# A decoder layer on one core: VectorE's order in the expert tiles, GpSimd's last copy of rows, and 258 columns read in place of 272

## The chip, the cores and the metric

The kernel runs on one core of one Trainium2 chip. The metric is the device time of one execution in microseconds (us), as the median of several runs. Engines are named as in the profile: PE is TensorE (PEld its weight loads), DVE is VectorE, ACT is ScalarE, POOL is GpSimd, SP is SyncE; a name with a q behind it is that engine's sequencer, which issues DMAs.

## The reference

The input is 128 batches of 128 tokens with 256 features. Each batch goes through causal self-attention (16 heads of 64), a layer norm, masked cross-attention (16 heads of 16) and another layer norm. The last part is a mixture of experts over all 16384 tokens, twice (two groups of 32 experts, each token to 2 experts of each group):

```python
logits = x2 @ router_w
expert_weights, expert_indices = lax.top_k(softmax(logits), 2)
xs = x2[tok]                                   # rows sorted by expert
ys = ragged_dot(silu(gate) * up, wd, group_sizes) * flat_w[order][:, None]
out_g = zeros_like(x2).at[tok].add(ys)
...
x = layernorm(x + (out0 * 2 + out1 * 2) / 4)
```

gate and up are `ragged_dot(xs, wg)` and `ragged_dot(xs, wu)` with 256 x 128 weights, wd is 128 x 256; all is float32.

## The kernel before

The program has two blocks, one after the other.

**The first block** takes the batches in a software pipeline of 137 iterations, each of four sub-steps s = 0 to 3. Attention of batch b is worked on in iteration b and later ones; with lag 4 its tokens' places in the experts' lists are made, and with lag 5 its rows are sent. GpSimd's part of that is three functions. `token_rows(b)` copies the batch's normalised rows into `xrow[b % 2]` four times (one for each of a token's four choices) and adds a code; it first waits until the scatters of batch b - 2, which read the same buffer, have landed (`placed`). `open_blocks(b)` makes the block numbers (`rows_of`) from which VectorE's `place_tokens(b)` makes the rows' places. `scatter(b, s)` issues four indirect DMAs, two at s = 2 and two at s = 3, that write the rows (272 columns: 256 features, code, owner and padding) to the arrays `xs_d` in HBM, sorted into tiles of 128 rows of one expert. After the last batch SyncE loads half of the first group's expert weights (`first_half(sp, 1)`), and the block ends when every engine is done; the second block starts on all engines behind that.

**The second block** takes 576 tiles (288 for each group) in steps n = 0, 1, 2 ..., one tile a step, again as a pipeline. In step n:

- SyncE loads tile n's rows into one of 10 buffers `xg` once the code of tile n - 10 is read (`to_made`). Being only issue work, it runs ahead of the others. It also stores finished sums, and loads later expert weights (`LATER`: eight experts in five pieces, one every third step from steps 60, 110 and 160, and four experts each at steps 299 and 303).
- TensorE transposes tile n (L1200), multiplies tile n - 1 by gate and up (L1208), works out in registers where tile n's weights lie (`find_weights`; in every fourth step it also loads a word from memory), transposes h of tile n - 2 (L1219) and multiplies tile n - 3 by the down weights (L1224).
- ScalarE copies tile n's transpose (L1236), then h's transpose of tile n - 2 (L1240), then makes `gate` of tile n - 1 (L1244), then may issue two DMAs for a combine.
- GpSimd issues the indirect DMA that writes tile n - 3's result `y` to its tokens' rows of `y_d` (L1155), with the places in `to`.
- VectorE copies y of tile n - 3 out of PSUM (L1290) into one of four buffers, and makes the places `to` (L1298) and h of tile n - 1 (L1300).

When all tiles that a batch can have rows in are written, the batch is combined: in every second step n (from step 46 to 300, and from 334 on) VectorE has a sum before y (L1285, first sum, of rows that ScalarE's DMA of four steps earlier brought) and one after y (L1293, second sum). In the second group it also has the layer norm's statistics: `bn_stats` (L1305) and the final scaling (L1319) in the steps without sums, `bn_aggr` and the variance (L1311, L1313) in those with sums, and GpSimd has a power (L1151). All this comes in the order in which the code lists it; each engine takes its instructions in that order.

A y buffer is free when its write of four tiles earlier has landed (`y_out`); the two PSUM banks of y are reused every second step; h's PSUM input is freed by h.

Of the kernel before, what the change touches and what calls it, by code (L numbers as in the profile page):

```python
# [25 lines left out]
ALU = mybir.AluOpType  # L26
# [3 lines left out]
P = 128  # L30
D = 256
# [12 lines left out]
HID = 128  # L44
# [50 lines left out]
def wait(eng, sem, value):  # L95

    if isinstance(value, int) and value <= 0:
        return
    eng.wait_ge(sem, value)
# [55 lines left out]
def decoder_layer(nc, xT, x, cT, mask, wq, wk, wv, wo, xwq, xbq, xwk, xbk, xwv, xbv, xwo, xbo,  # L155
                  r0, g0, u0, d0, r1, g1, u1, d1, out):
    NB = x.shape[0]
    N = NB * P
    TILES = NB * TOPK + E
    NT = NGRP * TILES  # L160
    PACK = 4
    SPARE = 4
    ROW = D + 16
    CODE, OWNER = D, D + 1
    x2_d = nc.dram_tensor("x2_d", (N, D), F32).ap()
    xs_d = [nc.dram_tensor(f"xs{g}_d", (TILES * P, ROW), F32).ap() for g in range(NGRP)]
# [5 lines left out]
    with keep:  # L172
# [48 lines left out]
        with ExitStack() as one:  # L221
            def sb(name, shape, dt=F32):
                return tile(one, name, shape, dt)
# [177 lines left out]
            with nc.Block() as block:  # L401
# [71 lines left out]
                def _(pool):  # L473
# [44 lines left out]
                    def iteration(t):  # L518
                        for s in range(NG):
                            lag, g = taken(s)  # L520
                            if s == 2 and (t.live(1) or t.live(3)):
                                pool.wait_ge(var_ready, t.item(1) + 1)
                                nc.gpsimd.tensor_tensor(rs[:, :], spread_v[:, :], minus_half[:, :], ALU.pow).then_inc(rsqrt_ready, 1)
                            if t.live(lag):
                                c = slice(2 * g, 2 * g + 2)
                                pool.wait_ge(y_high, t.item(lag) * NG + (g + 1))
                                nc.gpsimd.tensor_tensor(yT_p[1][:, c, :], yT[:, c, :], yT_p[0][:, c, :].bitcast(F32), ALU.subtract).then_inc(y_split, 1)  # L527
                            if s == 0 and t.p % 2 and t.live(-3):
                                p = t.pair_slot(-3)
                                pool.wait_ge(x_high, t.pair(-3) + 1)  # L530
                                nc.gpsimd.tensor_tensor(xT_p[p][1][:, :, :, :], xT_s[:, :, :, :], xT_p[p][0][:, :, :, :].bitcast(F32), ALU.subtract).then_inc(x_split, 1)  # L531
                                if t.among(-3, 1):
                                    for n in (2, 3):
                                        weight_low(nc.gpsimd.tensor_tensor, pool, n)
                            if s == 1 and t.live(1):
                                keys, n = xkD[:, t.two(1), :, :, :], t.item(1)
                                pool.wait_ge(moved["xk"], n + 1)
                                for m in range(KC):
                                    last = nc.gpsimd.tensor_tensor(keys[:, m, 1:XHALF, :], spread(keys[:, m, 0, :], 1, XHALF - 1),
                                                                   spread(own_head[:, 1:XHALF], 2, P), ALU.mult)  # L540
                                last.then_inc(xk_others, 1)
                                pool.wait_ge(xk_others, n + 1)
                                nc.gpsimd.tensor_tensor(keys[:, :, 0, :], keys[:, :, 0, :], spread(own_head[:, 0:1], 2, P).broadcast_to([P, KC, P]),
                                                        ALU.mult).then_inc(xk_ready, 1)
                            if s == 2 and t.live(1):
                                pool.wait_ge(x1_ready, t.item(1) + 1)
                                nc.gpsimd.tensor_tensor(x1b[t.two(1)][:, :], x1[t.two(1)][:, :], xbo_s[:, :], ALU.add).then_inc(x1b_ready, 1)
                            if s == 1 and t.live(4):
                                token_rows(t.item(4))
                            if s == 2 and t.live(4):  # L550
                                open_blocks(t.item(4))
                            if t.live(5):
                                scatter(t.item(5), s)

                    def open_blocks(b):

# [24 lines left out]
                    def scatter(b, s):  # L581

                        p = b % 2
                        if s == 2:
                            pool.wait_ge(xrow_ready, b + 1)
                            pool.wait_ge(place_ready, b + 1)
                            pool.wait_ge(cleared, CLEAR * clears_for(b))
                        for j in SCATTERS[s]:
                            nc.gpsimd.indirect_dma_start(  # L589
                                xs_d[j // TOPK][:, :], bass.IndirectOffsetOnAxis(ap=place[p][:, j:j + 1].bitcast(U32), axis=0),  # L590
                                xrow[p][:, j, :], None).then_inc(placed[p], 16)
# [444 lines left out]
        with ExitStack() as two:  # L1036
# [19 lines left out]
            packs = [flat[:, i * (NT // PACK):(i + 1) * (NT // PACK)] for i in (0, 1)]  # L1056
            tabs = sb("tabs", [1, NT // PACK], I32)
            spare_no = sb("spare_no", [P, SPARE])
            xg_s = [sb(f"xg{q}", [P, ROW]) for q in range(NX)]
            to = sb("to", [P, NTO], I32)  # L1060
            xgT = [sb(f"xgT{q}", [P, KC, P]) for q in (0, 1)]
            gate_s = [sb(f"gate{q}", [P, HID]) for q in (0, 1)]
# [32 lines left out]
            def combined(n, group=None):  # L1095

                for g in range(NGRP):
                    b, odd = divmod(n - g * TILES - FIRST, 2)
                    if not odd and 0 <= b < NB and group in (None, g):
                        return g, b, g * NB + b  # L1100
                return None

            with nc.Block() as block:
                @block.sync
                def _(sp):
                    for g in range(NGRP):
                        sp.dma_start(owners[:, g * TILES:(g + 1) * TILES, :],
                                     xs_d[g].rearrange("(n p) d -> p n d", p=P)[0:1, :, CODE:OWNER + 1]).then_inc(owners_in, 16)

                    def iteration(t, n):  # L1110
                        for first, count, piece, after in LATER.get(n, ()):
                            if piece == 0:
                                if n == LAST_CHUNK:
                                    sp.wait_ge(y_made, TILES)
                                sp.wait_ge(moe_in, after * CHUNK_LOAD)
                            load_piece(sp, 1, first, count, piece)
                        if t.live(0):
                            q, g = n % NX, n // TILES
                            wait(sp, to_made, n - NX + 1)
                            sp.dma_start(xg_s[q][:, :], xs_d[g][(n - g * TILES) * P:(n - g * TILES + 1) * P, :]).then_inc(xg_in[q], 16)  # L1120
                        done = combined(n - STORE)
                        if done:
                            g, b, k = done
                            p = k % NS
                            if g:
                                sp.wait_ge(out_ready, b + 1)
                                sp.dma_start(out[b, :, :], sums[p][:, :]).then_inc(stored[p], 16)
                            else:
                                sp.wait_ge(sum_ready, k + 1)
                                sp.dma_start(acc_d[b * P:(b + 1) * P, :], sums[p][:, :]).then_inc(stored[p], 16)  # L1130

                    tiles(iteration)
                    for q in range(NQ):
                        sp.wait_ge(y_out[q], 16 * (NT // NQ))
                    for p in range(NS):
                        sp.wait_ge(stored[p], 16 * (NGRP * NB // NS))
# [122 lines left out]
                def _(dve):  # L1259
# [16 lines left out]
                        return weight[:, b, g * TOPK + j:g * TOPK + j + 1]  # L1276

                    def iteration(t, n):
                        now = combined(n - COMBINE)
                        if now:  # L1280
                            g, b, k = now
# [9 lines left out]
                        if now:  # L1291
                            dve.wait_ge(part_ready, k + 1)
                            v.scalar_tensor_tensor(s[:, :], rows[:, k % NR, 1, :], weight_of(g, b, 1), s[:, :], ALU.mult, ALU.add).then_inc(sum_ready, 1)  # L1293
                        if t.live(1):
                            q, m = t.slot(1), t.item(1)
                            dve.wait_ge(gate_in, m + 1)
                            wait(dve, ht_made, t.item(2))
                            v.tensor_tensor(to[:, m % NTO:m % NTO + 1], xg_s[m % NX][:, CODE:CODE + 1], spare_no[:, m % SPARE:m % SPARE + 1],  # L1298
                                            ALU.max).then_inc(to_made, 1)
                            v.tensor_tensor(h_s[q % 2][:, :], gate_s[q % 2][:, :], GB[q % 2][:, HID:2 * HID], ALU.mult).then_inc(h_in, 1)  # L1300
                        full = combined(n - COMBINE - 1, 1)
                        if full:
                            g, b, k = full
# [66 lines left out]
```

## Time and profile before

| | |
|---|---|
| Median of 3 runs | 4887.19 us (4886.07 to 4888.65) |
| The profiled execution's own time | 4894.84 us |
| Its span, first to last instruction | 4893.1 us |
| First block | 0 to about 3750 us |
| Second block | about 3750 to 4893 us |
| Busy over the span: PE, PEld, DVE, ACT, POOL | 97%, 81%, 77%, 70%, 55% |

The busy shares are means over two blocks with different work. Times of rows are microseconds from the start of the span. A row of the timeline has the start, the duration, engine, line, operation and operands (out <- in), and in brackets how long the engine had been idle and what ended that, as inferred from semaphores. Matmuls are pipelined, and their ends are modelled: a group of matmuls overlaps the next, so distances between starts tell more than durations.

### The profile page before, as it was taken

To read this page: it belongs to the slowest core of one execution; us is meant where nothing else is said; L and a number is where in the kernel's file an instruction comes from. 1 tells how busy PE (TensorE), PEld (TensorE's weight loads), DVE (VectorE), ACT (ScalarE), POOL (GpSimd) and SP (SyncE) were. 2 spreads that over 40 slices of the span, in tenths; PEclk is the share of its full clock that TensorE was granted. 3 is DMA by queue.
4 is the path that set the end of the run, shared out by engine and by line. 5 is a ranking of instruction groups with operands and counts; after the bars stand their busy time and mean duration, and the time that the engine had idled before them with its cause. 6 is when DMAs were issued, how large, how long until landed. Compare 5 with 4: busy or idle time off the path is not lost. (4 is left out here: it accounts for less than half of the span.)

```text
span 4893.1 us, 133371 instructions
## 1 busy us (share of the span) xinstructions
PE 4755.2 (97%) x38848; PEld 3976.5 (81%) x38848; DVE 3782.2 (77%) x18828; ACT 3412.7 (70%) x13380; POOL 2712.7 (55%) x3750
## 2 busy tenths in 40 slices
PE   7999999999999999999999999999995999999998
PEld 6888888888888888888888888888874766676665
DVE  4888888888888888888888888888883455547777
ACT  5788888878878888887887888788783444444443
POOL 3455555555555555555555555555554555556666
PEclk9999999999999999999999999999997999999999
DMA  4121111112112111211211211121125799878888
GB/s 137 62 69 61 58 65 64 57 60 69 58 58 67 62 58 64 65 58 57 67 62 57 67 64 58 61 67 58 58 78 162 255 299 298 273 246 270 273 273 255
DMA packets 477157, 556.18 MB, mean 114 GB/s; under 512 B 55602, under 2 KB 407860, under 8 KB 475956
## 3 DMA queue, kind: packets, MB, share of 16 engines
q1 hardware_dynamic: 350516, 300.08, 19.9%
q0 software_dynamic: 52224, 146.87, 8.0%
q10 hardware_dynamic: 73728, 100.70, 6.8%
q8 instruction: 352, 5.77, 0.5%
q14 instruction: 337, 2.76, 0.2%
HBM read 270.08 MB, written 277.35 MB: 112 GB/s over the span
## 5 line engine op out<-in xcount | busy, mean ns | idle before, releaser
L527 POOL TENSOR_TENSOR yTl<-yT,yTh 128x256 fp32r<-128x256 f32 x512 | 381.7, 745 | 910.7 <-DVE yTh L979 907.6
L756 ACT ACTIVATE prob<-prob,negmax 128x128 f32<-128x128 f32 x2048 | 799.0, 395 | 102.5 <-DVE negmax L827 98.3
L1155 POOL DMA_INDIRECT y_d<-y,to x576 | 593.2, 1030 | 464.6 <-DVE y L1290 447.8
L756 ACT ACTIVATE xprob<-xprob,xnegmax 128x128 f32<-128x128 f32 x2048 | 792.9, 392 | 1.6 <-DVE xnegmax L827 1.6
L1208 PE MATMUL bank<-moe,xgT 128*128 x2304 | 594.6, 381 | 0.0
L589 POOL DMA_INDIRECT xs_d<-xrow,place x512 | 515.9, 1008 | 128.1 <-issue 128.1
L1290 DVE COPY y<-bank 128x256 f32<-128x256 f32 x576 | 244.5, 424 | 407.4 <-PE bank L1224 290.0
L827 DVE CUSTOM_DVE_ANT_0 prob<-bank,causal 128x128 f32<-128x128 f32 x2048 | 471.7, 286 | 34.0 <-PE bank L695 20.9
L774 ACT COPY probT<-bank 128x512 f32<-128x512 f32 x512 | 300.0, 586 | 248.0 <-PE bank L705 181.1
L827 DVE CUSTOM_DVE_ANT_0 xprob<-bank,xmask 128x128 f32<-128x128 f32 x2048 | 470.5, 286 | 1.2 <-remote 1.2
L837 DVE TENSOR_TENSOR prob<-prob,inv 128x512 f32<-128x512 f32 x512 | 438.9, 857 | 20.2
L616 PE MATMUL bank<-xT0h,wqkv 128*128 128x256 f32 x2048 | 401.6, 289 | 26.8 <-POOL xT0l L531 26.0
L1240 ACT COPY hT<-bank 128x128 f32<-128x128 f32 x576 | 153.2, 266 | 391.0 <-issue 208.8
L1208 PEld LDWEIGHTS bank<-moe,xgT 128*128 128x128 f32 x2304 | 394.0, 191 | 30.2 <-issue 0.3
L1236 ACT COPY xgT<-bank 128x256 f32<-128x256 f32 x576 | 214.3, 372 | 292.6 <-PE bank L1200 146.4
L616 PE MATMUL bank<-xT1h,wqkv 128*128 128x256 f32 x2048 | 400.7, 288 | 0.0
L1224 PE MATMUL bank<-moe,hT 128*128 x1152 | 392.9, 423 | 0.5
L807 ACT COPY yT<-bank 128x256 f32<-128x256 f32 x512 | 190.4, 372 | 290.2 <-PE bank L731 189.2
L756 ACT ACTIVATION_READ_ACCUMULATOR prob<-prob,negmax 128x1 f32 x2048 | 391.2, 191 | 0.0
L756 ACT ACTIVATION_READ_ACCUMULATOR xprob<-xprob,xnegmax 128x1 f32 x2048 | 391.0, 191 | 0.0
L844 DVE TENSOR_TENSOR xprob<-xprob,xinv 128x512 f32<-128x512 f32 x512 | 373.2, 729 | 17.6
L686 PE MATMUL bank<-kT,qT 64*128 64x128 f32 x4096 | 366.3, 297 | 0.4 <-DVE xnegmax L827 0.4
(180 smaller groups left out, 14188.3 us busy)
## 6 DMA issues: line engine op xcount, KB each, us to landing
xg<-xs_d SPq DMA_DIRECT2D x576, 136.0 KB
xs_d<-blank SPq DMA_DIRECT2D x248, 272.0 KB
rows<-y_d ACTq DMA_DIRECT2D x256, 256.0 KB
xT_s<-xT SPq DMA_DIRECT2D x128, 128.0 KB
x<-x SPq DMA_DIRECT2D x128, 128.0 KB, 2.0
cT<-cT SPq DMA_DIRECT2D x128, 128.0 KB
x_d<-x SPq DMA_DIRECT2D x128, 128.0 KB, 2.0
sums<-x_d ACTq DMA_DIRECT2D x128, 128.0 KB
```

Source lines behind the costliest of these rows:

```text
L527: nc.gpsimd.tensor_tensor(yT_p[1][:, c, :], yT[:, c, :], yT_p[0][:, c, :].bitcast(F32), ALU.subtract).then_inc(y_split, 1)
L589: nc.gpsimd.indirect_dma_start(xs_d[j // TOPK][:, :], bass.IndirectOffsetOnAxis(ap=place[p][:, j:j + 1].bitcast(U32), axis=0), xrow[p][:, ...
L616: last = nc.tensor.matmul(out_ap, lhs(a, k), rhs(b, k), start=(i == 0), stop=(i == len(todo) - 1))
L686: last = nc.tensor.matmul(SELF_SCORES[h], qT[HALVES[h % 2], t.slot(0), c, :], kT[HALVES[h % 2], key_slot(t.slot(0)), c, :], start=True, st ...
L756: last = nc.scalar.activation(dst[:, h, :], dst[:, h, :], ACT.Exp, bias=src_bias[:, h:h + 1], scale=-1.0, accum_out=acc[:, h:h + 1])
L774: nc.scalar.copy(probT[:, :, :].rearrange("p h q -> p (h q)"), T[:, :]).then_inc(probT_in, 1)
L827: last = nc.vector.tensor_tensor_reduce(dst[:, h, :], heads[h], bias[:, :], -1.0, float("inf"), ALU.add, ALU.min, least[:, h:h + 1])
L837: nc.vector.tensor_tensor(prob[s % 2][:, :, :], prob[s % 2][:, :, :], spread(inv[:, :], 2, P), ALU.mult).then_inc(normed, 1)
L844: nc.vector.tensor_tensor(xprob[s % 2][:, :, :], xprob[s % 2][:, :, :], spread(xinv[:, :], 2, P), ALU.mult).then_inc(xnormed, 1)
L1155: nc.gpsimd.indirect_dma_start(y_d[:, :], bass.IndirectOffsetOnAxis(ap=to[:, m % NTO:m % NTO + 1].bitcast(U32), axis=0), y_s[q][:, :], Non ...
L1208: last = nc.tensor.matmul(GB[q % 2][:, 0:2 * HID], xgT[q % 2][:, k, :], moe_cols[:, bass.ds(gate_up + k * 2 * HID, 2 * HID)], start=(k == ...
L1224: nc.tensor.matmul(YB[q % 2][:, 0:D], hT_s[q % 2][:, :], moe_cols[:, bass.ds(down, D)], start=True, stop=True).then_inc(y_made, 1)
```

## The change

Three edits. In the second block, VectorE makes `to` and h of tile n - 1 as the first work of step n; before, both came behind the first sum, y and the second sum. In the first block, `token_rows` of the last batch moves from s = 1 (ahead of `open_blocks` of the same batch and of the scatters of the batch before) to s = 3 of the same iteration, behind both. And the load of a tile's rows reads 258 of the 272 columns; the `xg` buffers are 258 wide. The rows in HBM keep 272 columns.

```diff
-                            if s == 1 and t.live(4):
+                            if s == 1 and t.live(4) and t.item(4) < NB - 1:
                                 token_rows(t.item(4))
                             if s == 2 and t.live(4):
                                 open_blocks(t.item(4))
                             if t.live(5):
                                 scatter(t.item(5), s)
+                            if s == 3 and t.item(4) == NB - 1:
+                                token_rows(t.item(4))
...
-            xg_s = [sb(f"xg{q}", [P, ROW]) for q in range(NX)]
+            xg_s = [sb(f"xg{q}", [P, D + 2]) for q in range(NX)]
...
-                            sp.dma_start(xg_s[q][:, :], xs_d[g][(n - g * TILES) * P:(n - g * TILES + 1) * P, :]).then_inc(xg_in[q], 16)
+                            sp.dma_start(xg_s[q][:, :], xs_d[g][(n - g * TILES) * P:(n - g * TILES + 1) * P, 0:D + 2]).then_inc(xg_in[q], 16)
...
                     def iteration(t, n):
+                        if t.live(1):
+                            q, m = t.slot(1), t.item(1)
+                            dve.wait_ge(gate_in, m + 1)
+                            wait(dve, ht_made, t.item(2))
+                            v.tensor_tensor(to[:, m % NTO:m % NTO + 1], xg_s[m % NX][:, CODE:CODE + 1], spare_no[:, m % SPARE:m % SPARE + 1],
+                                            ALU.max).then_inc(to_made, 1)
+                            v.tensor_tensor(h_s[q % 2][:, :], gate_s[q % 2][:, :], GB[q % 2][:, HID:2 * HID], ALU.mult).then_inc(h_in, 1)
                         now = combined(n - COMBINE)
...
                             v.scalar_tensor_tensor(s[:, :], rows[:, k % NR, 1, :], weight_of(g, b, 1), s[:, :], ALU.mult, ALU.add).then_inc(sum_ready, 1)
-                        if t.live(1):
-                            q, m = t.slot(1), t.item(1)
-                            dve.wait_ge(gate_in, m + 1)
-                            wait(dve, ht_made, t.item(2))
-                            v.tensor_tensor(to[:, m % NTO:m % NTO + 1], xg_s[m % NX][:, CODE:CODE + 1], spare_no[:, m % SPARE:m % SPARE + 1],
-                                            ALU.max).then_inc(to_made, 1)
-                            v.tensor_tensor(h_s[q % 2][:, :], gate_s[q % 2][:, :], GB[q % 2][:, HID:2 * HID], ALU.mult).then_inc(h_in, 1)
                         full = combined(n - COMBINE - 1, 1)
```

## Rows read from the trace of the kernel before

**Rows 1.** Busy time by stretch, h of L1300 alone: stretch, DVE (count), clock, DMA share, GB/s

```profile
3780.00:3838.00 58.00, 9.25 (x33) 1.00 0.50 161
3840.00:4330.00 490.00, 69.48 (x250) 1.00 0.92 293
4400.00:4870.00 470.00, 66.65 (x240) 1.00 0.85 270
```

**Rows 2.** Waits of the weight loads, 4400 to 4870: us in total, times, longest

```profile
PEld bank L1219 <- DVE h L1300: 49.4, 116, 0.9
PEld bank L1219 <- issue: 31.9, 64, 0.5
```

**Rows 3.** Timeline of a step with sums, first group

```profile
4000.12 0.27 PE L1219 MATMUL bank<-ident,h 128*128 128x128 f32 x1
...
4000.59 0.28 ACT L1244 ACTIVATE gate<-bank 128x128 f32<-128x128 f32 x1
...
4000.91 0.42 DVE L1290 COPY y<-bank 128x256 f32<-128x256 f32 x1 [0.59 <-issue]
4000.93 1.03 PE L1208 MATMUL bank<-moe,xgT 128*128 x4
...
4001.25 0.47 DVE L1293 SCALAR_TENSOR_TENSOR sums<-rows,weight,sums 128x256 f32<-128x256 f32 x1
...
4001.72 0.28 DVE L1300 TENSOR_TENSOR h<-gate,bank 128x128 f32<-128x128 f32 x1
...
4002.05 0.33 PE L1219 MATMUL bank<-ident,h 128*128 128x128 f32 x1
```

**Rows 4.** Timeline of steps without sums; five L1219 in all, three shown

```profile
3786.45 0.27 PE L1219 MATMUL bank<-ident,h 128*128 128x128 f32 x1
...
3788.12 0.27 PE L1219 MATMUL bank<-ident,h 128*128 128x128 f32 x1
...
3793.53 0.27 PE L1219 MATMUL bank<-ident,h 128*128 128x128 f32 x1
```

**Rows 5.** Groups of instructions, 3700 to 4890: count, busy, mean ns, idle before

```profile
L1155 POOL DMA_INDIRECT y_d<-y,to x576 | 593.2, 1030 | 464.6 <-DVE y L1290 447.8 <-issue 16.8
...
L1151 POOL TENSOR_TENSOR rstd<-ve,half 128x1 f32<-128x1 f32 x128 | 73.7, 575 | 8.8 <-DVE ve L1313 6.2
...
L1311 DVE BATCH_NORM_AGGREGATE mv<-stat 128x2 f32<-128x6 f32 x128 | 21.7, 169 | 0.0
```

**Rows 6.** Chain of the second block: start, us, what

```profile
3961.77 7.34 DMA rows<-y_d
...
4331.29 5.76 DMA y_d<-y,to
```

**Rows 7.** Busy time by stretch, all engines: stretch, PE, PEld, DVE, ACT, POOL, clock, DMA, GB/s

```profile
3960.00:3980.00 20.00, 19.51 (x97) 14.33 (x94) 11.62 (x44) 8.54 (x31) 9.92 (x10) 1.00 1.08 383
...
4100.00:4200.00 100.00, 97.05 (x462) 69.83 (x461) 55.11 (x204) 41.68 (x153) 54.84 (x51) 1.00 0.89 273
```

**Rows 8.** Timeline of POOL at the end of the first block

```profile
3723.09 0.96 POOL L589 DMA_INDIRECT xs_d<-xrow,place  x1 [0.30 <-issue]
3729.26 1.04 POOL L578 COPY xrow<-x 128x1024 f32<-128x1024 f32 x1 [5.21 <-DMA xs_d<-xrow,place]
...
3732.78 1.07 POOL L589 DMA_INDIRECT xs_d<-xrow,place  x1 [0.25 <-issue]
...
3741.75 0.96 POOL L589 DMA_INDIRECT xs_d<-xrow,place  x1 [0.30 <-issue]
3749.99 0.15 POOL L1140 IOTA spare_no<- 128x4 f32 x1 [7.28 <-POOLq L401]
```

**Rows 9.** Timeline of DVE there

```profile
3733.04 0.17 DVE L929 TENSOR_SCALAR place<-rank_b 128x4 int32<-128x4 f32 x1
```

**Rows 10.** Busy time by stretch there, columns as in rows 7

```profile
3738.00:3740.00 2.00, 0.00 (x0) 0.00 (x0) 0.00 (x0) 0.00 (x0) 1.70 (x2) 0.50 1.09 411
...
3742.00:3744.00 2.00, 0.00 (x0) 0.00 (x0) 0.00 (x0) 0.00 (x0) 0.71 (x1) 0.50 0.41 144
```

## The prediction

> **What bounds the kernel.** I read the page first: PE is busy nearly everywhere, but the second block moves far more data and has its own rhythm, so I took the blocks apart. The count of h per stretch gives the step time, since h is made once a tile. Without sums the step is 58/33 = 1.76 us; with sums it is 490/250 = 1.96 us in the first group and 470/240 = 1.96 us in the second [rows 1]. So a step with its share of the sums costs 0.2 us more, though PE does the same work in it, at full clock.
>
> The timeline says why. In the step with sums that starts at L1219, 4000.12, gate is ready at 4000.87, but VectorE then copies y (4000.91), adds the second sum (4001.25) and only then makes h (4001.72 to 4002.00). PE's next L1219 starts at 4002.05, right behind [rows 3]. The matmuls ahead of it (L1208, started 4000.93) are four passes of 256 columns, about 0.87 us by their spacing in steps without a gap: the sum of the distances of a gapless step is 1.68 us, and without sums L1219 does follow L1219 after 1.67 us [rows 4]. Here it took 1.93 us, 0.25 us late [rows 3]. The gap has a second price: the weight load of L1219 was not made under L1208, and what hangs on it shifts, which I estimate from the difference below. Four steps without sums take 3793.53 - 3786.45 = 7.08 us, or 1.77 a step: three of about 1.68 and one of about 2.04 us, in which PE's register work with its load is behind L1208 [rows 4]. With sums four steps take 4 x 1.96 = 7.84. The 0.76 us between them are two late h, so one costs 0.38 us: 0.25 us late, and 0.13 us for the weight load and the instructions behind it.
>
> The waits name h for 116 idles of L1219's load and "issue" for 64 [rows 2]. I read most of "issue" as h too, because the row shown in [rows 3] is such a start 0.05 us after h's end; only the register step is PE's own.
>
> **Edit 1, h first.** What moves: `to` and h are ahead of sum 1, y and sum 2 in each of the 576 steps. Nothing is added or removed. Let T be the start of L1219 in a step. Gate ends at T + 0.75 [rows 3]; h, with `to` ahead of it, then runs about T + 0.9 to T + 1.2. It is wanted when L1208 is over, at T + 1.68, and 0.15 us sooner for a hidden weight load: ready in both. Behind it, by full durations, sum 1 (0.48, as the second) ends at T + 1.7, y (0.42) at T + 2.1, sum 2 (0.47) at T + 2.6 [rows 3]. The next gate is there at T + 1.77 + 0.75 = T + 2.5, so the next h is at most 0.1 us later than it could be, and 0.3 us ahead of its need. In the second group `bn_aggr` (0.17 us) and the variance (about as long) come behind sum 2 [rows 5]: the next h ends up to 0.4 us later, just at the edge. By the start to start distance of y and sum 2 (0.34 us against 0.42 of duration [rows 3]) there is some 0.2 us more room. I take no stall, and keep 0.1 us in each of 121 step pairs, 12 us, as the bound above.
>
> The work passed over: y comes up to 0.9 us later in its step. Waiting on it are GpSimd's write, PE's L1224 two steps later (3.5 us, no matter), and the y buffer. One trip of a buffer is y 0.42, start of the write about 0.3 behind it, landing up to 5.76 us after that start [rows 6]: 6.5 us, against 4 x 1.77 = 7.1 us after the change and 7.84 before. GpSimd's own work for two steps is 2 x 1.03 + 0.58 = 2.6 us, with some 0.25 us of issue each 3.2, of 3.54 [rows 5]. Both fit, with little left. Rows for sum 1 took 7.34 us from issue at worst [rows 6]; they have four steps and, now, one h more, 7.1 + 0.4 us. SyncE sees `to_made` earlier, if anything, and stays over seven steps ahead.
>
> So the stretches with sums go to the rate without them. There are 254 + 242 = 496 steps from 46 to 300 and from 334 to 576: 496 x (1.96 - 1.77) = 94 us saved. From the other side: 248 late h at 0.38 give 94 us too. If only the visible 0.25 us goes it is 62 us.
>
> **What the faster steps collide with.** A step moves 273 GB/s x 1.96 us = 535 KB [rows 7], less 128 x 56 B = 7 KB by edit 3, 528 KB. At 1.77 us that is 298 GB/s, below the 383 GB/s that 20 us of this block carried [rows 7]. Where eight experts' weights (3.15 MB) come in over 12 steps, it would be 298 + 148 = 446 GB/s: 63 GB/s too many for 21 us, 1.3 MB, 3.5 us of backlog. Four such loads cost at most 14 us and, if the buffers take it up, nothing. I take 5 us. The Trainium skill, "DMA: Bandwidth & Descriptors", section "Where 436 GB/s comes from", puts the HBM limit of a core at about 358 GB/s; this trace carried 383 in a stretch, so the measurement decides. By 358 the four loads would cost an estimated 21 us.
>
> **Edit 2, the last copy.** Before, GpSimd was free at 3724.05, waited 5.2 us for the scatters of batch 125 to land, copied (3729.26), made the block numbers, and issued eight scatters from 3732.78 to 3742.71 [rows 8]. Copy and code take 1.3 us, so the block numbers took from 3730.5 to 3732.5, 2.0 us. Now: block numbers 3724.1 to 3726.1, four scatters of batch 126 at 1.27 us each from 3726.4 to 3731.3, by when the awaited landing (3729.2) is past; copy and code to 3732.6; four scatters of batch 127 from 3732.8 to 3737.6. Their places are 0.7 us of VectorE work behind landing and block numbers (3732.5 to 3733.2 before [rows 8, 9]), so ready at about 3730. GpSimd ends 5.1 us sooner. But weights are loading at 411 GB/s until about 3740, and what is left (144 GB/s in 3742 to 3744) was the last scatters alone [rows 10]. Moved up, those 288 KB still need 0.7 us at 411 GB/s behind what was moved up to 3742, so at worst the last landing is 1.3 us sooner, and more where the engines were not full. So 1.3 to 5.1 us less; I take 3.6, above the middle, since a scatter takes its turn beside the weights' queue. The next block starts 7.3 us behind the last scatter now [rows 8], with nothing else late.
>
> **Edit 3, 258 columns.** 1032 B a row in place of 1088: 7 KB of 535 a step, 1.3% of the DMA's load. No wait for `xg` is on the path, so 0 by itself. No row shows a 1032 B piece. Bounds: a gain of nothing, and a loss if such a piece is dearer (rival C).
>
> **Sum.** 94 + 3.6 - 5 = 93 us. The profiled execution took 4894.84 us, so 4802 in its own time; the median of the runs is 7.65 us lower, so 4794 us.
>
> **Rivals.** A, the y buffers and DMA bind: with landings near 6.3 us a buffer's trip is 7.1 us and each step above 1.77 is theirs. Against: 5.76 is among the longest pieces in the chain, and it fell in a weight load. For: 0.92 and 0.85 of share are busy already [rows 1]. If the step comes to 1.85 us, 496 x 0.11 = 55 us are saved: 4829. The Trainium skill, "DMA: Bandwidth & Descriptors", section "Latency and other measured facts", gives HBM latency as 0.2 us on average and 2 us at high load, which is the direction of this rival; the 5.76 us row was under load and can't tell its share.
>
> B, "issue" is what it says: register work holds L1219 and only the 116 of 180 idles named after h go [rows 2]: 0.64 x 94 = 60 us, 4824. Against it stands h's end just before the start [rows 3].
>
> C, slower: a 1032 B piece costs more than one of 1088. A tile's rows are 128 pieces, 8 on each of 16 DMA engines. The engines are busy 0.89 x 1.96 = 1.74 us a step, and have shown a share of 1.08 at most [rows 7]; the step becomes longer than 1.96 when busy time passes 2.12 us, that is at 0.37 us more, 47 ns a piece. At 80 ns more it would be 2.38/1.08 = 2.20 us, 496 x 0.24 = 120 us slower: 5007 us. Nothing in the rows speaks for it.
>
> D, edit 1 does nothing, because PE has another hold on L1219 at the same time as h ends, which leaves only edit 2's 3.6 us, 4884, within what counts as no change. The starts 0.05 us behind h [rows 3] speak against it.
>
> **Chances.** Forecast 0.73; A 0.11; B 0.08; C 0.03; D 0.02; 0.03 for a saving beyond 100 us. The measurement of this kernel can tell about 0.2%, 10 us. The forecast's own range is 4784 to 4812 (12 us of edge, 14 of DMA above, all buffers sufficing and 5.1 us below). For 8 in 10 it reaches to A and B: 4782 to 4828. Faster by over 0.2% is 0.95, within 0.02, slower 0.03.
>
> **What would show it.** Right: h per stretch at 1.77 us a step in both stretches with sums; h's start 0.1 us behind gate's end; L1219 after L1219 by 1.68 us, except in the register step; DMA near 300 GB/s. Edit 2: last scatter at about 3736.6, the next block 2 to 5 us sooner. Wrong: y waiting for "DMA y_d" (A), L1219 still idle behind "issue" with h long done (B), `xg` named as a releaser of L1200 with a DMA share over 1 (C), or VectorE's chain from sum 1 to the variance running into the next h in the second group.

## The result

| | before | after |
|---|---|---|
| Median | 4887.92 us (4886.07 to 4890.55, 4 runs) | 4756.11 us (4750.5 to 4757.66, 4 runs) |
| Profiled execution's span | 4893.1 us | 4755.9 us |

The ratio is 0.9727, with a 95% interval of 0.9716 to 0.9739: 132 us faster. The forecast was 4794 us, 93 us faster, with a range down to 4782. Direction and place were right. The size was not: the time lies 26 us below the range.

The profile after, first h by stretch, h of L1287 alone (stretch, VectorE busy and count, clock, DMA share, GB/s). It answers to [rows 1]:

```profile
3766.00:3826.00 60.00, 10.09 (x36) 1.00 0.56 165
3845.00:4245.00 400.00, 66.02 (x236) 1.00 0.99 335
4410.00:4710.00 300.00, 49.00 (x175) 0.99 0.94 308
```

With sums a step takes 400/236 = 1.695 us in the first group and 300/175 = 1.714 us in the second; it took 1.96 [rows 1], and 1.77 was forecast. The first row is the surprise: it has no sums, and its step went from 1.76 us to some 1.64. The count alone, 60/36 = 1.67, is coarse in so short a stretch; 37 h start from 3768.7 to 3827.7, which is 1.64 us a step. The forecast expected nothing there.

The timeline of steps without sums, with the transpositions of h, two of their weight loads and one h, answers to [rows 4]:

```profile
3785.91 0.27 PE L1221 MATMUL bank<-ident,h 128*128 128x128 f32 x1
...
3787.54 0.27 PE L1221 MATMUL bank<-ident,h 128*128 128x128 f32 x1
...
3788.40 0.28 DVE L1287 TENSOR_TENSOR h<-gate,bank 128x128 f32<-128x128 f32 x1
...
3788.95 0.14 PEld L1221 LDWEIGHTS bank<-ident,h 128*128 128x128 f32 x1
3789.16 0.27 PE L1221 MATMUL bank<-ident,h 128*128 128x128 f32 x1
...
3790.67 0.14 PEld L1221 LDWEIGHTS bank<-ident,h 128*128 128x128 f32 x1
3790.79 0.27 PE L1221 MATMUL bank<-ident,h 128*128 128x128 f32 x1
...
3792.54 0.27 PE L1221 MATMUL bank<-ident,h 128*128 128x128 f32 x1
```

The distances are 1.63, 1.62, 1.63 and 1.75: four steps in 6.63 us against 7.08 [rows 4]. So 1.68 was not the length of PE's work, and of the 0.36 us that the register step had over the others 0.12 is left. The weight load at 3788.95 starts 0.21 us ahead of its transposition. In the kernel before, the same stretch reads as follows (timeline: VectorE's y copy and h, the weight loads of L1219 and the y matmuls of L1224):

```profile
3787.65 0.28 DVE L1300 TENSOR_TENSOR h<-gate,bank 128x128 f32<-128x128 f32 x1
...
3787.98 0.14 PEld L1219 LDWEIGHTS bank<-ident,h 128*128 128x128 f32 x1
...
3788.24 0.64 PE L1224 MATMUL bank<-moe,hT 128*128 x2
...
3788.92 0.42 DVE L1290 COPY y<-bank 128x256 f32<-128x256 f32 x1 [0.99 <-issue]
...
3789.32 0.28 DVE L1300 TENSOR_TENSOR h<-gate,bank 128x128 f32<-128x128 f32 x1
...
3789.95 0.14 PEld L1219 LDWEIGHTS bank<-ident,h 128*128 128x128 f32 x1 [0.39 <-DVE h L1300]
3789.97 0.30 PE L1219 MATMUL bank<-ident,h 128*128 128x128 f32 x1
```

h ended at 3787.93 and its weight load started 0.05 us later, 0.14 us ahead of the transposition and not 0.21. Even without sums h came at the moment when it was needed, since y was copied ahead of it. The lines show a loop that closes on itself: h ends (3787.93), PE transposes it (3788.12) and, next in its order, makes y (3788.24 to 3788.88), VectorE copies y (3788.92) and only then makes the next h, which ends at 3789.60. One round is 1.67 us, the 1.68 of the forecast. The last two lines are the register step. In a step with sums of the kernel after (answer to [rows 3]):

```profile
4002.28 0.27 PE L1221 MATMUL bank<-ident,h 128*128 128x128 f32 x1
...
4002.75 0.28 ACT L1246 ACTIVATE gate<-bank 128x128 f32<-128x128 f32 x1
...
4003.14 0.28 DVE L1287 TENSOR_TENSOR h<-gate,bank 128x128 f32<-128x128 f32 x1
...
4003.34 0.48 DVE L1294 SCALAR_TENSOR_TENSOR sums<-rows,weight,sums 128x256 f32<-128x256 f32 x1
...
4003.73 0.42 DVE L1299 COPY y<-bank 128x256 f32<-128x256 f32 x1
4003.77 0.14 PEld L1221 LDWEIGHTS bank<-ident,h 128*128 128x128 f32 x1
4003.98 0.27 PE L1221 MATMUL bank<-ident,h 128*128 128x128 f32 x1
```

h ends at 4003.42, 0.35 us ahead of its weight load; the step is 1.70 us. The waits from 3845 to 4710 answer to [rows 2]:

```profile
DVE y L1299 <- DMA y_d<-y,to: 29.5, 50, 2.3
...
PEld bank L1221 <- issue: 14.8, 51, 0.7
PEld bank L1221 <- DVE h L1287: 9.2, 22, 2.2
PEld bank L1202 <- DMA xg<-xs_d: 6.0, 3, 2.6
```

The idles of L1219's load were 62.3 us after h and 80.3 after "issue" in the same stretch of the kernel before; 9.2 and 14.8 are left. New is that y waits for landings, 29.5 us.

The sum over the block: 80 steps without sums x (1.77 - 1.64) = 10; 254 x (1.961 - 1.695) = 68; 242 x (1.961 - 1.714) = 60; 2.75 for edit 2 (below); less some 4 us for one stall at 4269 (tiles 299 to 303 took 10.8 us, four steps of 1.64 are 6.6). That is 137 us, the difference of the spans (137.2).

Edit 2 in the timeline of GpSimd (answer to [rows 8]):

```profile
3730.73 1.04 POOL L580 COPY xrow<-x 128x1024 f32<-128x1024 f32 x1
...
3732.26 1.07 POOL L591 DMA_INDIRECT xs_d<-xrow,place  x1 [0.28 <-POOL xrow L581]
...
3736.16 0.96 POOL L591 DMA_INDIRECT xs_d<-xrow,place  x1 [0.30 <-issue]
...
3747.24 0.15 POOL L1142 IOTA spare_no<- 128x4 f32 x1 [10.12 <-POOLq L401]
```

The last scatter ends 5.6 us sooner (3742.71 to 3737.12), the next block starts 2.75 us sooner (3749.99 to 3747.24).

### The profile page after: what moved, and what is told of

Read it like the earlier page. It is cut to its first block and busy times, and to the rows that moved or that the text cites. A ratio compares the mean times of both kernels' runs of the same rounds, so it can differ in the third digit from the quotient of the medians.

```text
span 4755.9 us, 133371 instructions
## 1 busy us (share of the span) xinstructions
PE 4638.7 (98%) x38848; PEld 3980.0 (84%) x38848; DVE 3780.3 (79%) x18828; ACT 3414.2 (72%) x13380; POOL 2690.5 (57%) x3750
## 5 line engine op out<-in xcount | busy, mean ns | idle before, releaser
L1157 POOL DMA_INDIRECT y_d<-y,to x576 | 563.1, 978 | 353.4 <-DVE y L1299 328.7
L1210 PE MATMUL bank<-moe,xgT 128*128 x2304 | 596.8, 382 | 1.3 <-issue 1.0
L1210 PEld LDWEIGHTS bank<-moe,xgT 128*128 128x128 f32 x2304 | 394.6, 191 | 33.6 <-issue 3.4
L707 PEld LDWEIGHTS bank<-ident,prob 128*128 128x128 f32 x2048 | 214.5, 140 | 174.3 <-issue 165.7
L523 POOL TENSOR_TENSOR rs<-spread_v,minus_half 128x2 f32<-128x2 f32 x130 | 94.8, 729 | 466.1 <-DVE spread_v L900 466.1
L1226 PE MATMUL bank<-moe,hT 128*128 x1152 | 357.7, 392 | 0.1
```

What stands on the lines that cost most here:

```text
L1157: nc.gpsimd.indirect_dma_start(y_d[:, :], bass.IndirectOffsetOnAxis(ap=to[:, m % NTO:m % NTO + 1].bitcast(U32), axis=0), y_s[q][:, :], Non ...
L1210: last = nc.tensor.matmul(GB[q % 2][:, 0:2 * HID], xgT[q % 2][:, k, :], moe_cols[:, bass.ds(gate_up + k * 2 * HID, 2 * HID)], start=(k == ...
L1226: nc.tensor.matmul(YB[q % 2][:, 0:D], hT_s[q % 2][:, :], moe_cols[:, bass.ds(down, D)], start=True, stop=True).then_inc(y_made, 1)
```

## The experiments

Two readings stood against each other. **F**, the forecast's: 1.77 us is PE's own step, so the missing 39 us lie in another edit. **M**: PE's queue is served in order, and whatever makes h come at its need and not ahead of it exposes what is queued around it, the y copy as well as the sums.

**e1_h_first**, edit 1 alone: the two hunks of VectorE's `iteration`, nothing else.

> The kernel before with the first edit alone (places and h ahead of sums and y on VectorE in every step). Theory M, formed on the two traces: PE's sequencer takes instructions in order and stops at the transposition of h; what is queued behind it (the next step's first weight load, and every fourth step the register load) is exposed as soon as h ends at the moment it is needed and not ahead of it, so y's copy ahead of h cost something in the steps without sums too. By it the first edit carries everything but edit 2's 2.8 us: about -129 us, 4759. Theory F, the forecast's: 1.77 us is PE's own step, the edit is worth 88 to 94 us, 4794 to 4800, and the other 40 us came from the second or third edit. Decides: below 4770 for M, above 4790 for F.

Measured 4760.32 us (4752.05 to 4763.89), ratio 0.9734 [0.9722, 0.9747]. Edit 1 is worth 129 us alone (130 by the ratio); F's sum falls.

**e2_last_copy**, edit 2 alone.

> The kernel before with the second edit alone (the last batch's row copy behind the block numbers). M: block 2's first GpSimd work stood 2.75 us sooner in the trace after, so -2.8 us, 4885.1, inside 0.2%. F: -3.6 us (-1.3 to -5.1) by the forecast, or up to -40 if the missing 39 us lie here.

Measured 4887.15 us, ratio 0.9996 [0.9987, 1.0005]: 2 us, less than can be told from nothing.

**e3_258_columns**, edit 3 alone.

> The kernel before with the third edit alone (258 columns of each sorted row read). M: 0 us, within 0.1% (4883 to 4893), because no wait of the trace before ends in a landing of these rows. The rival: the fourth part of the bytes of that queue matters for the landings of the others and some of the missing 39 us lie here, 4850 to 4880.

Measured 4889.69 us, ratio 1.0001 [0.9992, 1.001]: nothing.

**e4_h_before_sum2**. In the kernel before:

```diff
 y copy
+to, h
 second sum
-to, h
```

> The kernel before with places and h moved ahead of the second sum only: VectorE's order is first sum, y, h, second sum. In steps with sums only the second sum's delay of h is removed. M: h then ends where it ended in the steps without sums, right at the need, the exposed queue work stays, 1.797 us per step in place of 1.962: 496 x 0.165 = -82 us, about 4806, and some 46 us short of e1_h_first. F: both orders reach the same floor of 1.77, so this one is level with e1_h_first within 5 us. Decides: the gap to e1_h_first, over 30 us for M, under 10 for F.

Measured 4800.14 us (4797.46 to 4801.55), ratio 0.9818 [0.9805, 0.983]. The gap to e1_h_first is 40 us, and h's place ahead of y or behind it is all that differs: F falls with this too. Its h by stretch (columns as above):

```profile
3766.00:3826.00 60.00, 9.52 (x34) 1.00 0.48 154
3845.00:4245.00 400.00, 62.61 (x224) 1.00 0.97 324
4410.00:4710.00 300.00, 47.54 (x170) 1.00 0.93 303
```

1.76 us without sums, 1.79 and 1.765 with. This is what the forecast described: steps with sums at the old rate of those without. It comes to 89 us, beside the forecast's 94 for its first term. The kernel after did more, because it put h ahead of y too.

**n1_before_noload** and **n2_after_noload**, no register load in PE's queue, in the kernel before and in the one after:

```diff
-                        if t.p == 2 and t.u + 1 < NT // PACK:
-                            pe.reg_load(next_word, tabs[0:1, bass.ds(t.u + 1, 1)])
...
-                            find_weights(t, int(n >= TILES))
+                            find_weights(t, 0)
```

The second hunk takes one register instruction (`if group: pe.reg_alu(...)`) out of every step of the second group too. The first word read is another one (`tabs[0:1, 3:4]`).

> The kernel before without the register load that PE's queue does in every fourth step: the expert numbers stay those of the first word read, so all tiles are multiplied with the same four experts' weights. That part of the computation is changed; the number, shapes and order of all engines' work are the same. In the trace before every fourth step (the one with the load) is longer than its neighbour of the same kind: 2.04 against 1.68 us without sums, 2.37 against 2.09 with. M: the load is paid because PE's queue waited for h until the moment h was needed; without it those steps become like the others: 80 steps / 4 x 0.36 + 496 / 4 x 0.28 = 42 us, 4847. A rival, that the load costs nothing and the fourth step is long for a reason of its own (a bank, a wait of ACT): 4889.

> The kernel after without the register load, all tiles with the same four experts' weights as in n1_before_noload. M: after the first edit the queue passes h with time in hand and the load lies under the matmuls; steps without sums stay at 1.64. In steps with sums the step with the load has a mean of 1.82 against 1.68 to 1.72 around it, so up to 0.14 x 124 = 17 us may still be paid: 4739 to 4756, less than half of what n1 gains. The rival, that the load has the same price of 0.28 to 0.36 us in both kernels: 42 us, 4714.

Measured 4850.61 us (ratio 0.9924 [0.9906, 0.9942]) for the first, 38 us under its like, and 4742.9 us (0.9705 [0.9688, 0.9723]) for the second, 13 us under its own. By the ratios it is 37 us with some 9 to either side, and 11 with some 10: clearly dearer where h is late, while "three times" is a rough figure. By the traces, from h of tile 0 to h of tile 288, n1 is 21 us shorter than the kernel before and n2 is 3 us shorter than the one after. In this first group nothing but the load is left out. The rest of n2's gain lies in the second group, where the other register instruction is missing too, and how much of it is the load's isn't shown. The transpositions of h in n1, without sums:

```profile
3786.80 0.27 PE L1217 MATMUL bank<-ident,h 128*128 128x128 f32 x1
...
3788.48 0.27 PE L1217 MATMUL bank<-ident,h 128*128 128x128 f32 x1
...
3790.19 0.27 PE L1217 MATMUL bank<-ident,h 128*128 128x128 f32 x1
...
3791.86 0.27 PE L1217 MATMUL bank<-ident,h 128*128 128x128 f32 x1
...
3793.54 0.27 PE L1217 MATMUL bank<-ident,h 128*128 128x128 f32 x1
```

1.68, 1.71, 1.67, 1.68: the long step is gone, and 1.68 stays where the kernel after has 1.62 or 1.63. So there are two costs of an h at its need: the register load in one step of four, and 0.05 us in every step. With the load in place, the means from h to h of the four steps of a group, tiles 8 to 44, are 2.06, 1.68, 1.70 and 1.68 us before and 1.63, 1.67, 1.63 and 1.66 after; without it they are 1.68 to 1.71 in n1 and 1.63 each in n2.

**n4_e4_noload**, the order of e4 without the register load.

> e4_h_before_sum2 (y still ahead of h, 4800.14) without the register load, all tiles with the same four experts' weights as in n1_before_noload. It splits the 40 us between e4 and e1_h_first, where h ends at the need in the one and 0.27 us ahead of it in the other. M: the exposed load is most of it; the step with the load is 2.04 against 1.68 without sums and 1.92 to 1.97 against 1.71 to 1.74 with: 80 / 4 x 0.36 + 496 / 4 x 0.21 = 33 us less, 4767, some 24 us above n2_after_noload, which is the 0.05 us per step of late weight loads (576 x 0.05 = 29). If the y copy's place itself costs the 40 us and not the queue, this stays at 4790 to 4800.

Measured 4784.36 us (4782.06 to 4789.88), ratio 0.978 [0.9764, 0.9796]: 16 us less than e4 (19 by the ratios), where M said 33. The waits of n4, 3845 to 4710:

```profile
DVE y L1288 <- DMA y_d<-y,to: 41.7, 48, 2.5
...
PEld bank L1217 <- DVE h L1295: 28.9, 48, 2.1
```

In e4 y waited 23.8 us for landings, here 41.7, and as y is ahead of h there, such a wait delays h too: PE's weight loads for the transposition of h idle for 28.9 us after it. In e1_h_first y waits 34.5 us for landings in the same stretch, and these loads idle for 12.1 us after h.

By the ratios of n4 and n2, 0.0075 or 37 us remain between the two orders with no register load at all, some 3 of them edit 2's. M's "most of it is the load" was wrong. The steps say where the rest lies. From h to h they take 1.71 us in n4 and 1.63 in n2 without sums (3768 to 3828), 1.76 and 1.68 with sums in the first group (3845 to 4245), 1.74 and 1.67 in the second (4410 to 4710). The 0.07 to 0.08 us a step are there without sums as well, in a stretch in which y waits for no landing in n4. So most of it is the loop through y. That late landings cost more time with y ahead of h is argued from the waits and not shown.

What is left over the 1.64 us of steps without sums? (1.695 - 1.64) x 254 + (1.714 - 1.64) x 242 = 32 us. The next runs change the kernel after.

**l3_after_load_end** and **l5_after_load_odd**, the register load at another place:

```diff
 l3: find_weights without the load; behind the y matmuls of PE's step:
+                        if t.live(0) and t.p == 2 and t.u + 1 < NT // PACK:
+                            pe.reg_load(next_word, tabs[0:1, bass.ds(t.u + 1, 1)])
 l5: in find_weights:
-                        if t.p == 2 and t.u + 1 < NT // PACK:
+                        if t.p == 1 and t.u + 1 < NT // PACK:
```

> The kernel after with the register load moved from behind the gate and up matmuls to the end of PE's step, behind the y matmuls; nothing is left out. M: what is still paid for the load in steps with sums (up to 17 us) is paid because the queue meets L1221's wait right behind it; at the end of the step it lies under the y matmuls (0.60 us), so 0 to 17 us less, 4739 to 4756. If the queue has less in hand there than it had, 5 to 20 us more.

> The kernel after with the register load one step earlier in each four, so that it falls in a step of PE's whose sums are not due; nothing is left out. n2 left 13 us of it; the interval behind the step with the load is 1.81 where its like is 1.72, and the one a step earlier is 1.66. If the load is paid only where it meets late sums, 5 to 13 us less than 4756 (4743 to 4751); if it only moves, 4756.

Measured 4756.08 us (0.9727) and 4771.02 us (0.9746 [0.973, 0.9762]). Neither helps. l5 missed: it costs 9 us by its ratio, 15 by the medians. Its h shows the loss in the first group, 225 in 400 us against 236. It lies mostly in the step with the load, 1.97 us on average there where the same step of the kernel after takes 1.65; why it bears the load worse stays open.

**r6_after_y6** (6 y buffers, 8 xg buffers) and its control **r7_after_x8** (8 xg buffers alone):

```diff
-            NQ, NX, NTO, NR, NS = 4, 10, 8, 4, 8
+            NQ, NX, NTO, NR, NS = 4, 8, 9, 4, 8      r6; y_s and y_out by m % 6
+            NQ, NX, NTO, NR, NS = 4, 8, 8, 4, 8      r7
```

> The kernel after with 6 y buffers in place of 4 (and 8 xg buffers in place of 10, 9 columns of places, 6 spare blocks of rows in y_d, to make room and keep the writes apart). The forecast's rival A, buffers of y that are not free in time: VectorE waited 15.9 + 11.7 us for landings of y in the trace after. If those waits are on the path, 15 to 28 us less, 4728 to 4741. If they are covered by VectorE's slack or the transfers only queue elsewhere, within 5 us of 4756.

> The kernel after with 8 xg buffers in place of 10 and nothing else: the control of r6_after_y6, which came out at 4764.33 where 4728 to 4756 was expected. If the row reads' shorter lead cost those 8 us, this one stands at 4764 or above, and r6 less this one is what the y buffers give; if it stands at 4756, 6 y buffers cost 8 us themselves.

Measured 4764.33 us (0.9746 [0.9728, 0.9763]) and 4765.77 us (0.9745 [0.9732, 0.9758]). Both stand 9 us above the kernel after by their ratios, r6 outside its expectation and r7 as its first case had it. That is hardly more than the intervals, but both show it: two xg buffers fewer cost some 9 us, two y buffers more give nothing beside them. With six y buffers the waits of y for landings (29.7 us in r7, 3845 to 4710) are gone, and the time is the same. So with h ahead of them they are worth nothing that can be measured, at 8 xg buffers; 6 y buffers with 10 xg were not tried. PE's waits for rows in `xg`, 4.8 us in the kernel after, are 10.8 in r7 and 14.4 in r6: the lead of the row reads is what the faster step leans on.

**s2_after_split_sums**, the second sum in the next step:

```diff
-                        if now:                                  (behind y)
-                            second sum of now
+                        half = combined(n - COMBINE - 1)         (ahead of y)
+                        if half:
+                            second sum of half
```

> The kernel after with the two sums of a batch in two steps: the first ahead of y in one step, the second ahead of y in the next, in place of both in one step around y. The steps with sums still take 1.70 to 1.71 us against 1.64 without. If that is VectorE's lateness in the step that has both (0.95 us of sums beside 0.86 us of places, h and y), up to 0.06 x 496 = 30 us less, 4726. If it is the DMA engines (share 0.98 and 0.95, 329 and 308 GB/s in these stretches), within 5 us of 4756.

Measured 4759.79 us, ratio 0.973 [0.9717, 0.9743]: no gain. VectorE's pile of work in the step with both sums is not what holds the 32 us.

**d1_after_half_rows**:

```diff
-     act.dma_start(rows[:, k % NR, :, :]..., y_of_token[b * P:(b + 1) * P, g * TOPK * D:(g + 1) * TOPK * D])
+     act.dma_start(rows[:, k % NR, 0, :], y_of_token[b * P:(b + 1) * P, g * TOPK * D:g * TOPK * D + D])
```

> The kernel after with half of each batch's rows read: only the row of the token's first expert, which both sums use, so the second expert's part of the result is not computed. It takes 128 of about 1026 KB off the transfers of two steps, and no instruction off any engine. If the DMA engines bind the steps with sums (shares 0.98 and 0.95), these come down from 1.71 to near 1.65, about 25 to 30 us less, 4726 to 4731. If VectorE's lateness does, within 5 us of 4756. Both may hold in part.

Measured 4747.19 us (4745.23 to 4754.37), ratio 0.9709 [0.9696, 0.9722]: 9 us by either measure, with an interval that still overlaps that of the kernel after a little, and a third of what a DMA bind was to give. The second expert's rows are not read, so its part of the result is left out. Its DMA share fell from 0.99 to 0.93 in the first group:

```profile
3845.00:4245.00 400.00, 66.62 (x239) 1.00 0.93 299
```

with 239 h for 236. By this measure the DMA engines hold some 9 of the 32 us, and the register work at most 11 to 13 (n2). That the two add up was not tried together, and some 10 us stay open. One candidate was not tried: ScalarE waits for landings of y ahead of its DMA for a combine, and its next copy waits with it (waits of the kernel after, 3845 to 4710):

```profile
ACT xgT L1238 <- DMA y_d<-y,to: 112.3, 195, 1.4
```

**z1_after_spread_load**:

```diff
-                    LATER.setdefault(LAST_CHUNK + 4 * h, []).append(...)
+                    LATER.setdefault(LAST_CHUNK + 5 * h + piece, []).append(...)
```

> The kernel after with the last two weight loads (two times five pieces of 256 or 512 KB) issued one piece a step and not five in one step. In the trace after SP's queue issued no row reads from 4258.9 to 4263.2 and PE then waited for rows until 4268.93, with a clock of 0.91 in that stretch; tiles 299 to 303 took 10.8 us where 4 x 1.66 were due. If the burst of pieces is the cause, about 4 us less, 4752; if the bytes alone are, nothing.

Measured 4755.43 us (4745.81 to 4758.04), ratio 0.9718 [0.9705, 0.9731]: 0.7 us by the medians and 4 by the ratios, too little to tell from nothing. All engines, 4253 to 4273 (columns as in [rows 7]), the kernel after and then z1:

```profile
4253.00:4273.00 20.00, 17.80 (x87) 13.93 (x86) 10.18 (x38) 7.73 (x28) 8.85 (x11) 0.91 1.08 378
```

```profile
4253.00:4273.00 20.00, 18.83 (x99) 14.68 (x97) 10.77 (x42) 8.98 (x33) 11.32 (x12) 1.00 0.97 320
```

The clock kept its level and these 20 us held 12 matmuls more, of 9 a step, 1.3 steps or 2.2 us. But the stall was split and not removed: in z1 PE waited for rows twice, 0.67 us at 4268.66 and, just behind this stretch, 1.06 us at 4273.58 (timeline of z1), 1.7 us in all where the kernel after waited 2.2 at once:

```profile
4273.58 0.44 PE L1202 MATMUL bank<-ident,xg 128*128 128x128 f32 x2 [1.06 <-DMA xg<-xs_d]
```

No version that computes the whole was measurably faster than the kernel after.

## Why the forecast was too small

**What holds the kernel** was read rightly: PE starts its transposition of h when h is there, and the sums and y on VectorE ahead of h make it late. The "issue" idles, which the forecast mostly put down to h, fell with it, from 80.3 to 14.8 us, and to 2.1 us in e4, which keeps PE's register work.

**The step that failed** is the rate it took as PE's own: "three of about 1.68 and one of about 2.04 us, in which PE's register work with its load is behind L1208", and from it "the stretches with sums go to the rate without them". The rate without sums was itself set by h, through y. Measured with h ahead of y: 1.63 and one of 1.75. The first term of the sum, 94 us, is what e4 gives (89 us), an edit that frees h of the second sum alone. The change frees it of y too, for 40 us more (e1 against e4), some 8 us of them in the stretches where the forecast had nothing. The evidence was at hand: an instruction 0.05 us behind h's end was the forecast's sign of a late h in [rows 3], and the steps of [rows 4] show the same sign as soon as their h is read beside them (3787.93 and 3787.98 above). The 2.04 us are from L1200 to L1200 or from h to h; from L1219 to L1219 the same 7.08 us divide into 1.67, 1.85, 1.88 and 1.68, so the reading doesn't come out of the instruction that [rows 4] names.

**The working of h's new place** held: h starts 0.11 us behind gate's end (forecast 0.1), ready 0.35 us ahead of its weight load in the step shown. The forecast gave the next transposition at T + 1.77 and stopped there; its own figures, h ready at T + 1.2 and wanted by T + 1.53, said that the register step had time to spare.

**The price of a late h**, 0.38 us, was right as a difference of two kinds of step, and both kinds were slow.

**Contention**, 5 us (bound 14): 9 us by d1, inside the bound, though d1 takes bytes off every step with sums and the forecast's term was for the weight loads alone. The rates came to 335 and 308 GB/s where 298 was forecast, because the step is shorter, and one 20 us stretch carried 378 GB/s at a share of 1.08.

**The y buffers' trip**, "both fit, with little left": it was less than little: y waits 29.5 us for landings. r6 against r7 shows that this costs nothing measurable. The buffers that did matter in r7, those of `xg`, were not named.

**Edit 2**: 3.6 us forecast; 2.75 in the trace, inside 1.3 to 5.1; e2's 2 us can't be told from nothing. GpSimd's end 5.6 us sooner against 5.1. **Edit 3**: 0 forecast, 0 measured.

**Rivals.** A would have meant 1.85 us a step, it was 1.70. B had register work as a fixed hold on PE; it was a part of what went, since its price depends on h (38 us in n1, 13 in n2). C and D did not happen. The case with 0.03, a saving beyond 100 us, came true, and the forecast had no mechanism for it. The range's ends don't follow from its terms either: 94 + 5.1 with no loss to DMA gives 4788, where 4784 was said, and 94 - 12 - 14 + 1.3 gives 4818, where 4812 was said.

How PE's register work comes to cost more when h is late is read from the runs, not seen: no view lists these instructions. The order in the program is gate and up matmuls, register work, wait for h, transposition, y, and then the next step's. If the queue stops at that wait, it gets to the next register work only so long after h has ended. The rows agree. From the end of h to the next weight load of its transposition the register step takes 2.02 us before (3787.93 to 3789.95) and 1.99 after (3788.68 to 3790.67), nearly the same in both orders. The steps beside it have 1.73 us from h's end to the next such load before, where h ends 0.05 us ahead of its own load, and 1.90 after, where it ends 0.27 ahead. So in the rows shown the step with the load is 0.29 us over the others in the one and 0.09 in the other, about the 0.27 and 0.09 of n1 and n2. The Trainium skill, "Perfetto Trace Analysis", section "Tensor Engine Instruction (MATMUL, LD_WEIGHTS)", lets the sequencer go on as soon as a waiting instruction has been pushed into the wait queue. By that alone a late h would cost the register work behind it nothing; n1 against n2 (38 and 13 us) says that in this kernel it does cost.

## What to carry to other kernels

A stretch without the suspected delay is not the engine's floor: look in it too for an instruction that starts just behind its operand's end, 0.05 us here, and count every producer ahead of that operand. Follow it back: if it leads to the engine's own work of the step before, the step is a loop and not a floor. Put what the bounding engine waits for first on its producer, ahead of copies that themselves wait for DMA. PE's register work was hidden here only as far as its queue ran ahead; when a step with such work is longer than the others, ask first whether the queue had any lead.

## What the runs showed of the hardware

Leaving out the load of one word into a register of PE saved 38 us over 143 times, 0.27 us each, where the queue had no lead (n1), and 13 us, at most 0.09 each, where it had (n2). An idle of 0.39 us was put down to h (3789.95, above) though h had ended at 3789.60: it was the register step's. After PE had waited 2.20 us for rows (at 4268.93), the granted clock of 4253 to 4273 was 0.91 (1.00 up to 4268, 0.71 in 4268 to 4271, 0.58 in 4271 to 4273), and matmuls there ran partly at the lower of TensorE's two levels: four of L1210 took 1.89 us in place of 1.03.

```profile
4268.93 0.44 PE L1202 MATMUL bank<-ident,xg 128*128 128x128 f32 x2 [2.20 <-DMA xg<-xs_d]
...
4269.20 1.89 PE L1210 MATMUL bank<-moe,xgT 128*128 x4
```

With the last weight loads spread out, the waits were 0.67 and 1.06 us and the clock stayed at 1.00 (z1, 4253 to 4273 and 4273 to 4276).
